# The biases of two graph layers: rank-one products of TensorE replaced by constant matrices that VectorE adds, in a kernel of four chained network layers on one core

## The reference

```python
    def _L2_gnn_ref(x, adj, Wg0, bg0, Wg1, bg1, Wih, Whh, bih, bhh):
        h = jax.nn.relu(jnp.einsum('ts,bsh->bth', adj, x @ Wg0 + bg0))
        h = jax.nn.relu(jnp.einsum('ts,bsh->bth', adj, h @ Wg1 + bg1))
        # windows of 1 to 4 nodes go through LSTMs, whose last states replace nodes of h
```

## Time and profile before

| what | value |
|---|---|
| three executions | 1996.74, 1998.2, 2000.57 us (median 1998.2) |
| the profiled execution | 1997.27 us, span 1995.5 us |
| PE, DVE, ACT busy | 97%, 86%, 72% of the span |
| mean granted clock of TensorE | 0.995 |
| pass one, two, three begin at about | 7.5, 130.7, 223.9 us |

### The profile page before, as it was taken

One profiled execution on the slowest core, in us unless ns is written; L12 is line 12 of the kernel. 1 busy time (PEld: TensorE's weight loads), 2 busy tenths in 40 slices (PEclk: granted clock), 3 DMA queues, 4 the chain that ended last, 5 costly groups with the idle time before them and its releaser, 6 DMA issues.

```text
span 1995.5 us, 85613 instructions
## 1 busy us (share of the span) xinstructions
PE 1939.5 (97%) x37017; PEld 1732.8 (87%) x37017; DVE 1714.6 (86%) x4774; ACT 1442.2 (72%) x4475; POOL 188.2 (9%) x260
## 2 busy tenths in 40 slices
PE   7999889999999999999999999999999999999997
PEld 4554479999999999999999999999999999999996
DVE  6889887898898988898889889898889888988866
ACT  5767457767777777768777777777777877677777
POOL 2000110101101010101001010101010101111000
PEclk9999999999999999999999999999999999999999
DMA  8958200000100010000100010001000010000000
GB/s 301 337 191 296 80 23 3 13 13 3 45 14 13 3 39 9 17 9 3 45 13 13 3 45 14 13 3 45 3 24 3 3 45 14 13 3 13 3 3 24
DMA packets 36822, 87.79 MB, mean 44 GB/s; under 512 B 2416, under 2 KB 26992, under 8 KB 32752
## 3 DMA queue, kind: packets, MB, share of 16 engines
q1 hardware_dynamic: 34448, 67.88, 9.6%
q10 hardware_dynamic: 2016, 14.68, 2.3%
HBM read 52.15 MB, written 30.41 MB: 41 GB/s over the span
## 4 chain that ended last, share of the span: by engine, by line
PE 79%; ACT 5%; DVE 4%; issue 1%; POOL 0%; ACTq 0%; DVEq 0%
PE ps L1551 19%; PE ps L1580 11%; PE ps L1560 9%; PE ps L1365 8%; PE ps L1399 7%; PE ps L1587 6%; PE ps L1375 4%; PE ps L1407 3%; PE ps L468 2%; PE ps L1342 2%; ACT pool_mem L1738 2%; PE ps L1332 1%; PE ps L1639 1%; PE ps L1453 1%; PE ps L1607 1%; DVE stats L1861 1%
## 5 line engine op out<-in xcount | busy, mean ns | idle before, releaser
L1738 ACT ACTIVATE pool_mem<-ps,lstm_b 128x64 f32<-128x64 f32 (+2 forms) x2496 | 606.3, 364 | 148.0 <-PE ps L1587 102.7
L1551 PE MATMUL ps<-hl_a,w_hi 128*128 128x64 f16 (+1 forms) x3584 | 362.6, 206 | 1.8 <-DVE hl_a L2017 0.9
L1551 PE MATMUL ps<-hl_a,w_lo 128*128 128x64 f16 (+1 forms) x3584 | 362.1, 206 | 0.0
L1830 POOL TENSOR_TENSOR rstd<-mv,nhalf 128x2 f32<-128x2 f32 x224 | 173.9, 778 | 1592.2 <-DVE mv L1865 1592.2
L1551 PEld LDWEIGHTS ps<-hl_a,w_hi 128*128 128x128 f16 x3584 | 285.1, 98 | 6.3 <-DVE hl_a L2017 1.2
L1551 PEld LDWEIGHTS ps<-hl_a,w_lo 128*128 128x128 f16 x3584 | 284.1, 98 | 2.8
L1580 PE MATMUL ps<-pool_mem,w_hi 128*128 128x64 f16 (+2 forms) x3072 | 273.7, 200 | 0.0
L1580 PE MATMUL ps<-pool_mem,w_lo 128*128 128x64 f16 (+2 forms) x3072 | 273.7, 200 | 0.0
L1560 PE MATMUL ps<-hl_a,w_hi 128*128 128x64 f16 (+1 forms) x3584 | 234.0, 205 | 0.0
L1580 PEld LDWEIGHTS ps<-pool_mem,w_hi 128*128 128x128 f16 x3072 | 228.9, 98 | 2.7
L1580 PEld LDWEIGHTS ps<-pool_mem,w_lo 128*128 128x128 f16 x3072 | 227.8, 98 | 0.7
(11 more groups left out here) (255 smaller groups left out, 4765.5 us busy)
## 6 DMA issues: line engine op xcount, KB each, us to landing
xa<-in_x SPq DMA_DIRECT2D x32, 512.0 KB, 4.8
h_scratch<-pool_mem ACTq DMA_DIRECT2D x14, 1024.0 KB, 4.9
pool_mem<-h_scratch SPq DMA_DIRECT2D x14, 1024.0 KB, 6.6
pool_mem<-in_wpack SPq DMA_DIRECT2D x16, 704.0 KB, 6.1
out<-xb SPq DMA_DIRECT2D x16, 512.0 KB, 3.4
o_scratch<-act_in SPq DMA_DIRECT2D x14, 512.0 KB, 3.0
act_in<-o_scratch SPq DMA_DIRECT2D x14, 512.0 KB, 5.1
row<-in_rows SPq DMA_DIRECT2D x1, 1408.0 KB, 10.2
```

What stands on the lines that cost most here:

```text
L1551: nc.tensor.matmul(o, wk[part], toks[0][:, k], start=(g, m) == gms[0] and k == 0 and part == 0, stop=False, skip_group_check=True)
L1738: op = nc.scalar.activation(gates[s][h][:, g, m * w:(m + 1) * w], gate_place(s, h, g, m, w), ACT.Tanh, bias=lstm_b[:, bias:bias + 1], scal ...
L1830: nc.gpsimd.tensor_tensor(rstd[s][:, blocks(h)], mv[s][:, blocks(h), 1], nhalf[:, 0:HALF], ALU.pow)\
```

## The change

Layer one's bias is no longer added in PSUM. DVE, not ACT, takes gcn0's product, as the larger of product and `neg0`, where neg0 = -(row sum of adj) x b0, a matrix of nodes x features. That is the relu of product plus bias, less the bias term itself. What is missing goes through mix1 and gcn1 as a constant, which is put into `gcn_b` together with layer two's bias: features x nodes, 2 x (A_SUMS x (b0 W1) + SUMS x b1). DVE adds gcn_b to gcn1's product in two operations (gcn_bias) and writes h1_full; ACT then makes the float16 half from it with a relu, once, and DVE the low half by `(h1_full max 0) - high`, a new step gcn_low. Steps gcn0 leave ACT's list and enter DVE's.

The bias products L1369 and L1402, the SUMS product of the start, the tiles sums and gbias, ACT's copies and POOL's row work are gone. The set-up stands at the end of pass one (PE, DVE), with 9 filler products instead of 19, and in DVE's part of pass two's end. The matrix `scaled` is written again by DVE ahead of pass one's loop. In ORDER the lists of all four engines are written anew: at 48 of the 164 places of PE's repeated part another step stands than before, at 2 of POOL's 28. The steps of PE are the same.

The diff, cut to its core (of ORDER two pairs of lines as a sample):

```diff
 ORDER = {
     "PE": ("""
...
-1:cheb.1 0:cell3.0 1:conv.1 1:v.0 1:q.0 1:k.0 0:inp4.1 1:scores.0 1:turn_x1.1 0:inp4.0 1:v.1 1:q.1 1:k.1 0:inp5.0
+1:cheb.1 0:cell3.0 1:v.0 1:conv.1 1:q.0 1:k.0 0:inp4.1 1:scores.0 1:turn_x1.1 0:inp4.0 1:v.1 1:q.1 1:k.1 0:inp5.0
...
     "DVE": ("""
...
-1:norm_l1.0 0:hid10.1 0:cell9.0 1:mix1.1 0:hid9.0 0:turn_state.1 1:mix0.0 1:gcn1.1 0:norm_l2.1 0:cell10.0
+1:norm_g3.0 0:hid10.1 0:cell9.0 1:mix1.1 1:norm_l1.0 0:hid9.0 1:gcn1.1 0:turn_state.1 1:gcn_low.1 1:mix0.0
...
-        sums = sb("sums", [P, HALF * P], F16)
-        gbias = sb("gbias", [P, 2, DIM], F16)
+        neg0 = sb("neg0", [P, DIM])
+        gcn_b = sb("gcn_b", [P, KT, NODES])
+        b0_hl = sb("b0_hl", [P, 2, KT], F16)
...
-            SUMS = ps[1][:, 2, 0:P]
+            B_COL, B0_W1 = spare[:, 80:80 + 2 * KT], spare[:, 88:88 + KT]
+            A_SUMS, SUMS = (spare[:, (2 + j) * NODES:(3 + j) * NODES] for j in range(2))
+            b_col = setup[:, 24:24 + 2 * KT]
...
-                nc.gpsimd.memset(sums[:, :], 0.0)
-                nc.gpsimd.memset(gbias[:, :, :], 0.0)
...
-                pool.wait_ge(row_in, 16)
...
-                nc.gpsimd.tensor_scalar(scaled_row[:, 2:4, :], row[:, g0:g0 + 2, :], WSCALE, None, ALU.mult).then_inc(set_ok, 1)
...
-                act.wait_ge(step, 7)
-                for j in range(HALF):
-                    part = slice(j * P, (j + 1) * P)
-                    nc.scalar.copy(sums[0:1, part], SUMS[0:1, :])
-                    nc.scalar.copy(sums[64:65, part], SUMS[64:65, :])
-                    nc.scalar.copy(sums[32:33, part], SUMS[32:33, :]).then_inc(rows_ok, 1)
                 unit_high(0, 1)
...
-                nc.tensor.transpose(GCN, scaled, ident[:, :])
-                nc.tensor.matmul(SUMS, ones, at_bd[:, :], start=True, stop=True).then_inc(gcn_ps, 1)
+                nc.tensor.transpose(GCN, scaled, ident[:, :]).then_inc(gcn_ps, 1)
...
                 hidden(1, ROUNDS, range(HT))
+                pe.wait_ge(row_in, 16)
+                for layer in range(2):
+                    for j in range(KT):
+                        nc.tensor.matmul(B_COL[:, layer * KT + j:layer * KT + j + 1], row[0:1, g0 + layer, j * P:(j + 1) * P],
+                                         ones[0:1, 0:1], start=True, stop=True)
+                pe.wait_ge(gc_ok, 1)
+                nc.tensor.matmul(A_SUMS, ones, scaled[:, 0:NODES], start=True, stop=True)
+                nc.tensor.matmul(SUMS, ones, at_bd[:, 0:NODES], start=True, stop=True).then_inc(gc_ps, 1)
                 pe.wait_ge(hid_out[0], ROUNDS * HT + 1)
-                keep_clock(ps[0][:, 2, :], 19)
+                keep_clock(ps[0][:, 2, :], 9)
+                pe.wait_ge(gc_ok, 4)
+                for m in range(KT):
+                    for k in range(KT):
+                        product(B0_W1[:, m:m + 1], weight("wg1", k, m * P, P), (b0_hl[:, 0, k:k + 1], b0_hl[:, 1, k:k + 1]),
+                                k == 0, k == KT - 1)
...
-                dve.wait_ge(rows_ok, HALF)
-                for j in range(HALF):
-                    part = slice(j * P, (j + 1) * P)
-                    nc.vector.tensor_tensor(sums[32:33, part], SUMS[32:33, :], sums[32:33, part], ALU.subtract)
                 unit_low(0, 1)
...
+                nc.vector.tensor_scalar(scaled, at_bd[:, :], rsum, None, ALU.mult).then_inc(gc_ok, 1)
                 with dve.Fori(0, ROUNDS - 1) as r:
...
+                dve.wait_ge(gc_ps, 1)
+                nc.vector.tensor_copy(b_col, B_COL).then_inc(gc_ok, 1)
+                dve.wait_ge(gc_ok, 2)
+                nc.vector.tensor_scalar(b0_hl[:, 0, :], b_col[:, 0:KT], WSCALE, None, ALU.mult).then_inc(gc_ok, 1)
+                dve.wait_ge(gc_ok, 3)
+                nc.vector.scalar_tensor_tensor(b0_hl[:, 1, :], b_col[:, 0:KT], WSCALE, b0_hl[:, 0, :], ALU.mult, ALU.subtract)\
+                    .then_inc(gc_ok, 1)
                 dve.wait_ge(bn_pow, 1)
...
                 nc.vector.tensor_scalar(wa_f, WA, WSCALE, None, ALU.mult).then_inc(set2_ok, 1)
+                twice_b0w1, twice_b1 = setup[:, 28:28 + KT], setup[:, 30:30 + KT]
+                nc.vector.tensor_scalar(neg0[:, :], row[:, g0, :], rsum, -1.0, ALU.mult, ALU.mult)
+                nc.vector.tensor_scalar(twice_b0w1, B0_W1, 2.0 * UNSCALE * UNSCALE, None, ALU.mult).then_inc(gb_ok, 1)
+                nc.vector.tensor_scalar(twice_b1, b_col[:, KT:2 * KT], 2.0, None, ALU.mult).then_inc(gb_ok, 1)
+                for m in range(KT):
+                    dve.wait_ge(gb_ok, 1)
+                    nc.vector.tensor_scalar(gcn_b[:, m, :], A_SUMS, twice_b0w1[:, m:m + 1], None, ALU.mult).then_inc(gb_ok, 1)
+                for m in range(KT):
+                    dve.wait_ge(gb_ok, 3 + m)
+                    nc.vector.scalar_tensor_tensor(gcn_b[:, m, :], SUMS, twice_b1[:, m:m + 1], gcn_b[:, m, :], ALU.mult, ALU.add)
...
-                    if with_row is not None:
-                        for b in range(HALF):
-                            nc.tensor.matmul(tok(s, bank)[:, b, :], with_row[0], with_row[1], start=False, stop=False,
-                                             skip_group_check=True)
...
-                        if with_sums:
-                            nc.tensor.matmul(out[:, j, :], gbias[:, 1, m * P:(m + 1) * P], sums[:, :], start=False, stop=False,
-                                             skip_group_check=True)
...
                 def mix_h(s, n, h):
-                    pe.wait_ge(*taken.at(s, n, h, "gcn"))
+                    pe.wait_ge(*gcn_ok.at(s, n, h, "t"))
...
                 def high(s, n, h, which):
...
+                    dst = like_feat(FEAT_DST[which][s][:, 0, :, tokens(h)], which)
                     if which == "h1":
-                        nc.scalar.activation(h1_full(s, h), src, ACT.Relu, scale=2.0 * UNSCALE)
-                        func, scale = ACT.Relu, 2.0 * UNSCALE
+                        act.wait_ge(*gcn_ok.at(s, n, h, "full"))
+                        nc.scalar.activation(dst, h1_full(s, h), ACT.Relu).then_inc(feat_hi.of(s, h), 1)
...
-                def gcn_relu(s, n, h):
-                    act.wait_ge(*tok_ps.at(s, n, h, "gcn"))
-                    nc.scalar.activation(t[s][:, blocks(h), :], tok(s, BANK_B[h]), ACT.Relu, scale=UNSCALE)\
-                        .then_inc(taken.of(s, h), 1)
...
                 def low(s, n, h, which):
...
+                    if which == "h1":
+                        nc.vector.scalar_tensor_tensor(lo, h1_full(s, h), 0.0, hi, ALU.max, ALU.subtract)\
+                            .then_inc(feat_lo.of(s, h), 1)
...
+                def gcn_relu(s, n, h):
...
+                    dve.wait_ge(*tok_ps.at(s, n, h, "gcn"))
+                    nc.vector.scalar_tensor_tensor(t[s][:, blocks(h), :], tok(s, BANK_B[h]), UNSCALE,
+                                                   neg0[:, :].unsqueeze(1).broadcast_to([P, HALF, DIM]), ALU.mult, ALU.max)\
+                        .then_inc(gcn_ok.of(s, h), 1)
...
+                def gcn_bias(s, n, h):
...
+                    dve.wait_ge(*feat_ps.at(s, n, h, "h1"))
+                    for k in range(KT):
+                        op = nc.vector.scalar_tensor_tensor(by_batch(h1_full(s, h))[:, k], by_batch(feat(s, h, "h1"))[:, k],
+                                                            2.0 * UNSCALE,
+                                                            gcn_b[:, k, :].unsqueeze(1).broadcast_to([P, HALF_BATCHES, NODES]),
+                                                            ALU.mult, ALU.add)
+                    op.then_inc(gcn_ok.of(s, h), 1)
```

More of the change, by code:

```diff
@@ L103 @@
[L103 to L107 removed]
+0:turn_y.1 0:turn_y.0 1:turn_y.0 1:turn_y.1 0:cheb.1 0:conv.1 0:cheb.0 0:conv.0 0:turn_x1.1 0:v.1 0:q.1 0:k.1
@@ new lines @@
+1:cell10.0 1:inp9.1 0+gcn0.1 1:turn_state.0 1:cell9.1 0+gcn0.0 1:inp10.1 1:turn_xc.0 1:cell10.1 1:gat.0 0+mix1.1
+1:gat_keys.0 0+mix1.0 1:turn_state.1 0+gcn1.1 0+gcn1.0 1:turn_att.0 1:gat_mix.0 1:turn_xc.1 0+inp0.1 1+turn_y.0
+1:gat.1 0+inp0.0 1:gat_keys.1 0+inp1.1 1+cheb.0 0+inp1.0 1+conv.0 1:turn_att.1 0+inp2.1 1:gat_mix.1 0+inp3.1
+1+turn_y.1 0+inp2.0 0+cell3.1 0+inp3.0 1+turn_x1.0
+""", """
+1:cheb.1 0:cell3.0 1:v.0 1:conv.1 1:q.0 1:k.0 0:inp4.1 1:scores.0 1:turn_x1.1 0:inp4.0 1:v.1 1:q.1 1:k.1 0:inp5.0
@@ new lines @@
+0:gat.1 1:gcn0.0 0:gat_keys.1 0:turn_state.0 1:inp1.1 1:mix1.0 0:turn_att.1 0:gat_mix.1 0:turn_xc.0 1:gcn1.0
+0+turn_y.1 0:gat.0 1:inp0.0 0:gat_keys.0 1:inp2.1 1:inp1.0 0:turn_att.0 0+cheb.1 0:gat_mix.0 1:inp3.1 0+conv.1
+0+turn_y.0 1:inp2.0 1:cell3.1 0+turn_x1.1 1:inp3.0 0+cheb.0 0+v.1 0+conv.0 0+q.1 1:cell3.0 0+k.1 0+turn_x1.0
+0+scores.1 0+v.0 0+q.0 0+k.0 1:inp4.0 0+scores.0 0+turn_probs.1 1:inp5.0 0+attend.1 1:cell5.0 1:inp4.1 0+attn_out.1
+1:inp6.0 0+turn_probs.0 1:cell6.0 0+attend.0 1:inp5.1 0+turn_x2.1 0+attn_out.0 0+mlp_up.1 1:inp7.0 1:cell5.1
@@ L2106, in run @@
                         ln_shift(s, n, h)
+                    elif base == "gcn0":
```

(5 more changed lines are left out.)

439 lines of the change are left out of this document (209 added, 230 removed).

## The result

The changed kernel takes 1988.8 us, the median of five executions (1987.64 to 1990.46), beside 1996.93 us for the kernel before on the same chip (1996.74 to 2000.57). The ratio is 0.9955, interval 0.9944 to 0.9966: faster by 8 to 9 us where 11.6 were forecast. The profiled execution took 1990.46 us, its span is 1988.7 us, 6.8 us under the span before.

What follows compares the result with a forecast made beforehand. PE, busy 214.56 of 215.73 us a period, was taken as the bound; -13.2 + 1.4 + 0.6 - 0.4 = -11.6 us gave 1986.6 us against the 1998.2 median. Forecast 1983 to 1991 (0.52); 8-in-10 range 1980.5 to 1994.

Steps and rivals of the forecast that it cites:

- three signs of being wrong: Period not shrinking by 1.3 us; full-period waits of mix1 or cell inputs for DVE; ramp idle moving over 3 us.
- The products, -13.2 us: Graph layers on PE: 120 of 128 removed bias products save 0.11 us each; eight in the ramp count nothing.
- More idle time, +1.4 us: Full periods of pass three: work moved to DVE's queue adds 0.2 us of PE idle in each of seven.
- The order, 0 with bounds of -2 and +4 us: Rewritten lists: only 1.2 us of idle movable in full periods, more in the ramp; taken as 0.
- The slower rival: Hand-overs gcn0 to mix1, gcn1 to inp0: DVE becomes the bound, periods 1.3 us longer, 2008 us; chance 0.05.
- Half given back: Rival: new order costs ramp or tail 4 us, idle grows 0.5 us a period, 1992.7 us; chance 0.12.
- Weight loads as the limit: Rival: PE's weight loads set the price, products bring 12.5 instead of 14.1 us, 1988.1 us; chance 0.08.
- Ramp, +0.6 us: Ramp, 220 to 300 us: longer DVE chains cost 0.3 us for each of two halves, between 0 and 3.
- Start-up, -0.4 us: Kernel start: without the SUMS product gcn_t and what follows come 0.4 us earlier, or 0.
- The gaps, nothing: Between passes one and two, and two and three: new DVE operations stay covered by other waits, counted at nothing.
- The clock in the first gap: Rival: between passes one and two PE's clock falls after a wait with fewer fillers, +2.9 us, 1989.5 us; chance 0.05.

Runs made afterwards that it cites:

- e2: The kernel before, its order and set-up kept, with only the 128 bias products left out; 1988.5 us, ratio 0.9952.
- e9: The kernel before with the 128 bias products out and idle DVE reductions added that nobody waits for; 1994.68 us, ratio 0.9981.
- e11: The changed kernel in its own order with DVE's bias step out, ACT reading gcn1's product twice; 1990.1 us, ratio 0.9964.
- e12: The changed kernel with the old order in the repeated part and DVE's bias step out, relu still on DVE; 1987.94 us, ratio 0.9954.
- e5: The changed kernel with the first graph layer's relu back on ACT, that layer's bias missing; 1990.23 us, ratio 0.9953.
- e1: The changed kernel run again without edit, beside the kernel before; 1988.61 us, ratio 0.9952.
- e3: The changed kernel with the repeated part of all order lists taken from the kernel before; 1996.29 us, ratio 0.9988.
- e4: The kernel before, its work and bias products kept, in the changed kernel's order lists; 2002.44 us, ratio 1.0024.
- e6: The kernel before in the changed kernel's order lists, with the 128 bias products left out; 1992.46 us, ratio 0.9971.
- e8: The changed kernel with the old order in the repeated part and the first layer's relu back on ACT; 1998.36 us, ratio 0.9999.
- e10: The changed kernel with the old order in the repeated part, two steps of PE's list moved later; 2011.79 us, ratio 1.0073.
- e13: The changed kernel with the old order in the repeated part, two places around gcn1 ordered as in the changed lists; 1999.25 us, ratio 1.0006.

## Why the prediction was right, and where it was not

The time lies in the range, 2.2 us above the forecast, and "faster" was right. The saving is 3.5 us short of the forecast's (8.1 instead of 11.6 us by the medians); the time is nearer than that because the kernel before came out 1.3 us lower, at 1996.9, than the 1998.2 that the sum started from. The route there was only partly the forecast's. Of its three signs of being wrong two came: the period shrank by 0.36 us where at least 1.3 was asked, and mix1 waits for DVE in the full periods (0.5 us in three of them); the ramp's idle time moved by 1.0 us, less than 3. So the range was met partly by luck.

- *The products, -13.2 us: the step that failed.* "What is taken off PE comes off the time" rested on a PE that is busy for 214.56 of 215.73 us. Removed alone, the 128 products brought 9.6 us (e2), 1.2 us of 1.76 a period in the old order and 1.5 in the new. The starts 0.11 us apart were read rightly; what was wrong is that busy time with a latency of several products in flight hides waits below that latency, and that taking products away adds such waits (0.6 us a period in e2).
- *More idle time, +1.4 us: right by its own sign, wrong as a cost.* PE's listed idle rose from 1.17 to 1.33 us a period. The whole loss, from e2's 214.6 to the changed 215.4 us, is 0.8 us a period. DVE's load at e9's price, 0.13 x 6.1 us, gives 0.8 as well. That agreement does not settle it: e11, with some 3 us less of it, is no faster, and the new order has a price of its own.
- *The order, 0 with bounds of -2 and +4 us: far off as a term, and the one that decided.* It is worth -6.6 us or a little more to the new work and costs the old work +4.8. I had argued that it can move only the 1.2 us of idle time in a period. It held off a loss of 2.0 us a period by the bias step, at a price of its own of 0.5 (e11 beside e12).
- *The slower rival* named the place (gcn1 to inp0, a queue in order with work behind the step) and the sign to look for, waits of cell inputs for DVE. In the old order that is what comes: the period is 216.9 us, longer than before. It needed no full DVE, as I had it; DVE sat idle for 1.27 us just there. In the changed kernel it does not occur.
- *Half given back* (1992.7 us, 0.5 us a period more idle) comes nearest in that the periods give back part of the gain, but not in size or place. Of 1.76 us a period, 1.4 were given back, not 0.5, and mostly not as idle time; and the ramp and the tail did not lose 4 us, so the time is better.
- *Weight loads as the limit* gives 1988.1 us, close to the median by chance: e2's 9.6 us are no more 12.5 than 14.1. In the new order the products do bring 1.5 us a period, close to the loads' 1.57, but by line the distances at their own places shrank by 1.75 us there too, 0.11 each, and the rest was given back elsewhere. The Trainium skill (Perfetto Trace Analysis, Identifying the Most-Contended Engine) is right for this trace in that matmul busy time is no measure of headroom; the loads' share, 93% of a period, did not give the price either.
- *Ramp, +0.6 us.* PE's idle time from 220 to 300 us is 16.75 us instead of 15.75, in a window into which pass three enters 2.5 us later, and to round two the kernel gained 0.8 us in spite of a later start.
- *Start-up, -0.4 us.* gcn_t's operation came at 7.93 instead of 8.49 us, as forecast (8.1). The first product of pass one follows it: it comes at 14.60 to 14.73 us in the eight traces with the new set-up and at 15.01 to 15.27 us in the five with the old one. So the term is right where it was to arise; by pass three it can't be told from the spread of the starts below.
- *The gaps, nothing.* In the first, DVE's three new operations lie from 130.91 to 131.46 us, in the shadow of POOL's power. In the second, the row that answers to the earlier trace rows shows the cover shrunk from 2.23 to 1.13 us, not used up:
```profile
221.74 0.69 DVE L1078 BATCH_NORM_STATS2 bnst<-act_in 128x6 f32<-128x512 f32 x1 [1.13 <-ACT act_in L955]
```
- *The clock in the first gap* did fall, and pass three began 2.5 us later. But the change was not what decides it, as the section on the hardware shows; the forecast's reason (fewer fillers, a new wait) was wrong.

## What to carry to other kernels

A product taken off a full engine is worth the distance of its starts only if nothing in the stretch is waited for; time the bare removal first (here 9.6 of 14.1 us), because it tells the price before any work is moved. When work is moved to an engine with an ordered queue, ask what stands ready behind it while it waits: a step of 0.75 us, four times a period, cost 2.0 us a period where it blocked its queue, and nothing where the order had been written for it. Order and work belong together: change one alone, in either direction, and 5 to 7 us were lost here, and two hand-made moves that removed the wait in view made the kernel slower.

## What the runs showed of the hardware

The clock at the end of pass one. Mean granted clock in the stretch from 120 to 130 us (the column behind POOL's), before:
```profile
120.00:130.00 10.00, 10.00 (x53) 5.09 (x53) 5.62 (x11) 2.75 (x4) 1.05 (x1) 1.00 0.26 109
```
the changed kernel:
```profile
120.00:130.00 10.00, 10.00 (x51) 5.71 (x52) 5.04 (x8) 3.12 (x5) 0.00 (x0) 0.83 0.33 136
```
e2, whose first two passes are those of the kernel before:
```profile
120.00:130.00 10.00, 10.00 (x48) 5.05 (x48) 5.16 (x8) 2.99 (x5) 0.00 (x0) 0.83 0.31 129
```
and e12, whose first two passes are those of the changed kernel:
```profile
120.00:130.00 10.00, 9.39 (x61) 5.20 (x61) 6.05 (x19) 2.91 (x6) 1.05 (x1) 1.00 0.17 70
```
0.83 over 10 us is 3.4 us at 1.2 GHz, in a stretch in which PE is busy without a break in the listed time. The slow stretch costs half of that, 1.7 us: pass two's fillers begin at 133.11 us in the changed kernel and at 130.74 before, and 0.69 us of these 2.37 were there ahead of the fall, at the first small product that follows the loop of pass one (119.58 and 118.89 us). Of thirteen traces (e5's left out) eight show it (after, e1, e2, e3, e4, e6, e8, e9) and five do not (before, e10 to e13); both set-ups occur with it, and both without it. With it, the first add_y of pass three comes at 227.8 to 228.5 us with the old set-up and at 227.5 to 229.1 us with the new; without it, at 226.6 and at 224.7 to 226.7 us. So the set-up does not decide it and costs nothing that could be told, and the 2.5 us that the first comparison shows can't be put down to the change. What does decide it is not shown. The eight traces with the fall come to that small product at 118.98 to 119.58 us and the five without it at 117.96 to 118.89; runs that were taken together agree with each other (e1 to e4 have it, e10 to e12 do not); and no kernel was traced both with it and without. That a comparison of two single traces can be off by 2 us in 230 in this way, with an unchanged program in that stretch, I had not expected.

The second surprise is the price of free time: 5.5 us of DVE work that nobody waits for, in a period in which DVE idles for some 20, cost 0.7 us.
